# Attention of a four-layer kernel, step by step: one maximum, one step of scores and one of V in turn, with ScalarE writing all seeds

## The reference, cut to what matters

```python
N_HEADS = 16
HEAD_DIM = 64
q = (x @ Wq).reshape(b, s, N_HEADS, HEAD_DIM)
k = (x @ Wk).reshape(b, s, N_HEADS, HEAD_DIM)
v = (x @ Wv).reshape(b, s, N_HEADS, HEAD_DIM)
dot = jnp.einsum('bihd,bkhd->bhik', q, k)
w = jax.nn.softmax(dot / jnp.sqrt(jnp.float32(HEAD_DIM)), axis=-1)
a = jnp.einsum('bhij,bjhd->bihd', w, v)
return a @ Wo + bo
```

## Time and profile before

| what | us |
|---|---|
| median of three runs | 1858.48 |
| lowest and highest | 1855.24, 1868.66 |
| the profiled execution | 1866.86 |
| its span, first to last instruction | 1865.6 |
| PE busy in it | 1637.2 (88%) |
| POOL, DVE, ACT busy | 1306.1, 1302.3, 1154.1 |

### The profile page before, as it was taken

The page is one execution under the profiler, slowest core; times in us unless marked ns, Lnnn a source line. Parts: engine busy times, 40 slices in busy tenths (PEclk is TensorE's granted clock), DMA queues, the critical chain, the costliest instruction groups (busy, mean ns, idle before and its releaser), DMA issues.

```text
span 1865.6 us, 33807 instructions
## 1 busy us (share of the span) xinstructions
PE 1637.2 (88%) x12993; PEld 916.9 (49%) x12993; DVE 1302.3 (70%) x2075; ACT 1154.1 (62%) x1618; POOL 1306.1 (70%) x670
## 2 busy tenths in 40 slices
PE   3988863668999999999999999999999999995795
PEld 3767642654444444444444444444444444442475
DVE  2565667457777777777777777777777777763476
ACT  2455530355777777777777777777777777774323
POOL 2233331423998899998899998999998999995422
PEclk8587755778999999999999999999999999997698
DMA  8000000210000000000000000000000000000312
GB/s 244 3 3 4 3 1 8 61 44 1 1 1 1 1 1 1 1 1 1 1 1 1 1 1 1 1 1 1 1 1 1 1 1 1 1 1 25 101 40 74
DMA packets 33239, 29.72 MB, mean 16 GB/s; under 512 B 3676, under 2 KB 28752, under 8 KB 33080
## 3 DMA queue, kind: packets, MB, share of 16 engines
q1 hardware_dynamic: 24664, 19.38, 3.5%
q0 software_dynamic: 2496, 5.13, 0.8%
q10 hardware_dynamic: 5920, 3.04, 0.8%
HBM read 18.33 MB, written 9.21 MB: 15 GB/s over the span
## 4 chain that ended last, share of the span: by engine, by line
PE 61%; issue 12%; DVE 12%; ACT 7%; POOL 5%; DMA 1%; ACTq 1%; another core or an unknown queue 0%; POOLq 0%; DVEq 0%; SPq 0%
PE psum L1921 18%; PE psum L1906 13%; PE psum L1872 9%; DVE a_mx L2108 3%; ACT psum L2040 3%; POOL a_acc L2227 3%; PE psum L1887 2%; PE psum L1525 2%; PE psum L1929 2%; POOL y_rows L1090 1%; DVE a_Ql L2094 1%; PE psum L465 1%; ACT a_Qh L2002 1%; ACT a_Onh L2017 1%; PE psum L375 1%
## 5 line engine op out<-in xcount | busy, mean ns | idle before, releaser
L2227 POOL TENSOR_TENSOR a_acc<-a_acc,a_Pb 128x1024 f32<-128x1024 f32 x448 | 1065.8, 2379 | 108.4 <-ACT a_Pb L2025 52.7
L2108 DVE TENSOR_REDUCE a_mx<-psum 128x2 f32<-128x1024 f32 x512 | 622.0, 1217 | 194.6 <-PE psum L1872 191.4
L2025 ACT ACTIVATE a_Pb<-psum 128x1024 f32<-128x1024 f32 x512 | 496.8, 1023 | 296.3 <-PE psum L1906 291.1
L1921 PE MATMUL psum<-a_Pb,a_Vb 128*64 128x512 f32 x2048 | 494.1, 603 | 0.0
L2040 ACT ACTIVATE psum<-a_Mb 128x1024 f32<-128x1024 f32 x352 | 352.6, 1034 | 0.0
L1872 PE MATMUL psum<-a_Kh,a_Qh 64*128 64x512 f32 x1024 | 256.5, 491 | 26.1 <-DVE a_mx L2108 19.9
L1872 PEld LDWEIGHTS psum<-a_Kh,a_Qh 64*128 64x128 f32 x1024 | 103.1, 184 | 328.7 <-issue 305.6
L1921 PEld LDWEIGHTS psum<-a_Pb,a_Vb 128*64 128x64 f32 x2048 | 127.0, 136 | 222.5 <-issue 175.6
L1906 PE MATMUL psum<-a_Qh,a_Kh 64*128 64x512 f32 x1024 | 204.0, 394 | 1.8 <-ACT psum L2040 1.8
L1906 PE MATMUL psum<-a_Ql,a_Kh 64*128 64x512 f32 x1024 | 202.7, 390 | 0.0
L1906 PE MATMUL psum<-a_Qh,a_Kl 64*128 64x512 f32 x1024 | 202.7, 390 | 0.0
(11 more groups left out here) (389 smaller groups left out, 2013.8 us busy)
## 6 DMA issues: line engine op xcount, KB each, us to landing
x_rows<-att_raw ACTq DMA_DIRECT2D x2, 1483.5 KB, 25.4
g_w<-in_L_ffn_w_eDF_dram SPq DMA_DIRECT2D x2, 1408.0 KB, 8.7
r_W<-in_L_ffn_W_dram SPq DMA_DIRECT2D x1, 2048.0 KB, 14.1
r_tile_x<-x_rows SPq DMA_DIRECT2D x23, 64.5 KB
g_tile_x<-x_rows SPq DMA_DIRECT2D x23, 64.5 KB
y_all<-y_rows SPq DMA_DIRECT2D x4, 256.0 KB, 3.6
g_w<-in_L_ffn_w_eFD_dram SPq DMA_DIRECT2D x2, 512.0 KB, 9.4
g_xg<-y_rows SPq DMA_DIRECT2D x4, 256.0 KB, 3.9
```

Source lines behind the costliest of these rows:

```text
L1921: last = pe.matmul(ps[HEAD[h], B_O, :], b.Vb[:, p // 2 % 2, kc, at], b.Pb[:, step % BUFS, h * QT:(h + 1) * QT], start=(kc == 0), stop=(kc ...
L2025: act.activation(b.Pb[:, step % BUFS, :], ps[:, slot:slot + 2, :].rearrange("p a b -> p (a b)"), ACT.Exp, scale=SCALE).then_inc(S["probs"], 1)
L2108: v.tensor_reduce(b.mx[:, :, qc, quarter:quarter + 1], ps[:, bank:bank + 2, :], AX.X, ALU.max).then_inc(S[f"free{bank}"], 1)
L2227: g.tensor_tensor(b.acc[:, u, :], before, b.Pb[:, step % BUFS, :], ALU.add).then_inc(S["added"], 1)
```

## The change

The loop no longer goes by rounds of two steps but by single steps. In each step TensorE does the scores of the step, one maximum, the V products of the step two before, then the other job and the seed job where the step has one. The max jobs run further ahead: at step i of unit U it is job 7 + i of unit U+1 for i under 9 (AHEAD), and job i - 9 of unit U+2 from there on. In unit 0 the first seven steps have two maxima each, since nothing was made before the loop. ScalarE does an exp, then the seed of the step two ahead (which waits for that very exp), then copies; all seeds but the first of a unit are its own, and DVE has none. Jobs stand at steps 1 (k), 3 (q), 4 (sum), 11 (out), 14 (v and seed). The inversion stands at steps 4 to 7. The sizes, the matmuls and their number are the same.

```diff
--- before.py
+++ after.py
@@ -1672,51 +1672,49 @@
 NU = NT * P // QT
 PAIRS = 8
 UNITS = PAIRS * NU
-RN = NT // 2
-ROUNDS = UNITS * RN
-STEPS = 2 * ROUNDS
+STEPS = NT * UNITS
 BUFS = 8
 SCALE = 1.0 / float(np.sqrt(D))
 B_O, B_M, B_P = 4, 5, 7
 
 
-def misc_job(R):
-
-    U, d = R // RN, R % RN
+
+INVERT = (4, 5, 6, 7)
+
+AHEAD = 9
+
+
+def misc_job(step):
+
+    U, i = step // NT, step % NT
     p, qt = U // NU, U % NU
-    if d == 0 and p < PAIRS - 1:
+    if i == 1 and p < PAIRS - 1:
         return "k", p + 1, qt
-    if d == 1 and U:
+    if i == 3 and U < UNITS - 2:
+        return "q", U + 2
+    if i == 4 and U:
         return "sum", U - 1
-    if d == 4 and U < UNITS - 2:
-        return "q", U + 2
-    if d == 5 and U:
+    if i == 11 and U:
         return "out", U - 1
-    if d == 6 and p // 2 < PAIRS // 2 - 1:
-        return "v", p // 2 + 1, U % RN
+    if i == 14 and p // 2 < PAIRS // 2 - 1:
+        return "v", p // 2 + 1, U % 8
     return None
 
 
-def seed_job(R):
-    U, d = R // RN, R % RN
-    return ("seed", U + 1) if d == 7 and U < UNITS - 1 else None
-
-
-def max_jobs(R):
-
-    U, i = (R + 1) // RN + 1, (R + 1) % RN
-    return [("max", U, 2 * i + j) for j in range(2)] if U < UNITS else [None, None]
-
-
-
-SEED_DVE = (0, 5, 6, 7)
-
-
-def seeder(step):
-
-    if step % NT == 0 or step == 1:
-        return "pe"
-    return "dve" if step % 2 and (step // 2 - 1) % RN in SEED_DVE else "act"
+def seed_job(step):
+    U, i = step // NT, step % NT
+    return ("seed", U + 1) if i == 14 and U < UNITS - 1 else None
+
+
+def max_jobs(step):
+
+    U, i = step // NT, step % NT
+    first = NT - AHEAD
+    if U == 0 and i < AHEAD:
+        jobs = [(1, 2 * i), (1, 2 * i + 1)] if i < first else [(1, first + i)]
+    else:
+        jobs = [(U + 2, i - AHEAD) if i >= AHEAD else (U + 1, first + i)]
+    return [("max", *job) for job in jobs if job[0] < UNITS]
 
 
...
@@ -1888,39 +1882,35 @@
                                      start=(qc == 0), stop=(qc == 3), skip_group_check=True)
         end(last, 0)
 
-    def scores(R):
-        U, d = R // RN, R % RN
+    def scores(step):
+        U, kc, slot = step // NT, step % NT, 2 * (step % 2)
         p = U // NU
-        if d == 0:
-            freed(("seed", U))
+        if kc == 0:
             freed(("q", U))
             freed(("k", p, NU - 1))
-        for i in range(2):
-            kc, slot = 2 * d + i, 2 * i
-            at = slice(kc * P, (kc + 1) * P)
-            who, n = plan.seeded[2 * R + i]
-            if who != "pe":
-                pe.wait_ge(S[f"seeded_{who}"], n)
-            for n, (K, Q) in enumerate(((b.Kh, b.Qh), (b.Kh, b.Ql), (b.Kl, b.Qh))):
-                for h in range(2):
-                    last = pe.matmul(ps[:, slot + h, :], K[HEAD[h], p % 2, at], Q[HEAD[h], U % 3, :], start=False, stop=(n == 2), skip_group_check=True)
-            last.then_inc(S["scores"], 1)
-
-    def weigh(R):
-        U, d = R // RN, R % RN
+        if kc == 0:
+            freed(("seed", U))
+        elif step > 1:
+            pe.wait_ge(S["seeded"], seeds_of(step))
+        at = slice(kc * P, (kc + 1) * P)
+        for n, (K, Q) in enumerate(((b.Kh, b.Qh), (b.Kh, b.Ql), (b.Kl, b.Qh))):
+            for h in range(2):
+                last = pe.matmul(ps[:, slot + h, :], K[HEAD[h], p % 2, at], Q[HEAD[h], U % 3, :], start=False, stop=(n == 2), skip_group_check=True)
+        last.then_inc(S["scores"], 1)
+
+    def weigh(step):
+        U, kc = step // NT, step % NT
         p = U // NU
-        if d == 0:
-            freed(("v", p // 2, RN - 1))
+        if kc == 0:
+            freed(("v", p // 2, 7))
             if U:
                 pe.wait_ge(S["heads_out"], U)
-        for kc in (2 * d, 2 * d + 1):
-            step = NT * U + kc
-            pe.wait_ge(S["probs"], step + 1)
-            for h in range(2):
-                at = slice((p % 2) * P + h * D, (p % 2) * P + (h + 1) * D)
-                last = pe.matmul(ps[HEAD[h], B_O, :], b.Vb[:, p // 2 % 2, kc, at], b.Pb[:, step % BUFS, h * QT:(h + 1) * QT],
-                                 start=(kc == 0), stop=(kc == NT - 1))
-            last.then_inc(S["weighted"], 1)
+        pe.wait_ge(S["probs"], step + 1)
+        for h in range(2):
+            at = slice((p % 2) * P + h * D, (p % 2) * P + (h + 1) * D)
+            last = pe.matmul(ps[HEAD[h], B_O, :], b.Vb[:, p // 2 % 2, kc, at], b.Pb[:, step % BUFS, h * QT:(h + 1) * QT],
+                             start=(kc == 0), stop=(kc == NT - 1))
+        last.then_inc(S["weighted"], 1)
...
@@ -1960,25 +1950,21 @@
         if m % 2:
             values(0, m // 2)
     seed(0)
-    for _, U, m in max_jobs(-1):
-        maximum(U, m)
     for bank in range(NU + 1):
         pe.wait_ge(S[f"free{bank}"], plan.before[bank])
     pe.wait_ge(S["att_ready"], 1)
-    for R in range(ROUNDS):
-        late, early = max_jobs(R - 1)[1], max_jobs(R)[0]
-        if R and late:
-            maximum(*late[1:])
-        scores(R)
-        if early:
-            maximum(*early[1:])
-        if misc_job(R):
-            misc(misc_job(R))
-        if seed_job(R):
-            seed(*seed_job(R)[1:])
-        if R:
-            weigh(R - 1)
-    weigh(ROUNDS - 1)
+    for step in range(STEPS):
+        scores(step)
+        for _, U, m in max_jobs(step):
+            maximum(U, m)
+        if step > 1:
+            weigh(step - 2)
+        if misc_job(step):
+            misc(misc_job(step))
+        if seed_job(step):
+            seed(*seed_job(step)[1:])
+    weigh(STEPS - 2)
+    weigh(STEPS - 1)
     sums(UNITS - 1)
     output(UNITS - 1)
...
     def seed(step):
         U, slot = step // NT, 2 * (step % 2)
-        if plan.seeded[step][0] == "act":
-            bank, n = plan.at["seed", U]
-            act.wait_ge(S[f"free{bank}"], n)
-            act.wait_ge(S["probs"], step - 1)
-            act.activation(ps[:, slot:slot + 2, :].rearrange("p a b -> p (a b)"), b.Mb[:, U % 2, :], ACT.Copy).then_inc(S["seeded_act"], 1)
+        if step % NT == 0:
+            return
+        bank, n = plan.at["seed", U]
+        act.wait_ge(S[f"free{bank}"], n)
+        act.wait_ge(S["probs"], step - 1)
+        act.activation(ps[:, slot:slot + 2, :].rearrange("p a b -> p (a b)"), b.Mb[:, U % 2, :], ACT.Copy).then_inc(S["seeded"], 1)
...
@@ -2055,24 +2041,22 @@
     for qt in range(NU):
         keys(0, qt)
     queries(1)
-    for j in range(RN):
+    for j in range(8):
         values(0, j)
     guard(0)
-    for R in range(ROUNDS):
-        U, d = R // RN, R % RN
-        probs(2 * R)
-        probs(2 * R + 1)
-        if seed_job(R):
+    for step in range(STEPS):
+        U, i = step // NT, step % NT
+        probs(step)
+        if seed_job(step):
             guard(U + 1)
-        for step in (2 * R + 2, 2 * R + 3):
-            if step < STEPS:
-                seed(step)
-        key = misc_job(R)
+        elif step + 2 < STEPS:
+            seed(step + 2)
+        if i == 1 and U:
+            heads_out(U - 1)
+        key = misc_job(step)
         if key and key[0] in "qkv":
             {"q": queries, "k": keys, "v": values}[key[0]](*key[1:])
-        if d == 0 and U:
-            heads_out(U - 1)
-        if d == 3 and U:
+        if i == 8 and U:
             normalised(U - 1)
     heads_out(UNITS - 1)
...
@@ -2167,30 +2143,24 @@
         maximum(0, m)
     dve.wait()
     negate(0)
-    for _, U, m in max_jobs(-1):
-        maximum(U, m)
-    for R in range(ROUNDS):
-        U, d = R // RN, R % RN
-        late, early = max_jobs(R - 1)[1], max_jobs(R)[0]
-        if R and late:
-            maximum(*late[1:])
-        if d == 7 and U < UNITS - 1:
+    for step in range(STEPS):
+        U, i = step // NT, step % NT
+        if i == AHEAD and U < UNITS - 1:
             negate(U + 1)
-        if U and d in (2, 3):
-            invert(U - 1, 2 * d - 3)
-        if U and d == 4:
+        for _, unit, m in max_jobs(step):
+            maximum(unit, m)
+        if i == 2 and misc_job(step - 1):
+            keys(*misc_job(step - 1)[1:])
+        if i == 3 and misc_job(step):
+            queries(U + 2)
+        if U and i in INVERT:
+            invert(U - 1, INVERT.index(i))
+        if U and i == 8:
+            normalise(U - 1)
+        if U and i == 10:
             normalised_low(U - 1)
-        if early:
-            maximum(*early[1:])
-        if U and d in (1, 2):
-            invert(U - 1, 2 * d - 2)
-        if 2 * R + 3 < STEPS:
-            seed(2 * R + 3)
-        key = misc_job(R)
-        if key and key[0] in ("q", "k", "out"):
-            {"q": queries, "k": keys, "out": output}[key[0]](*key[1:])
-        if U and d == 3:
-            normalise(U - 1)
+        if U and i == 11:
```

34 lines of the change are left out of this document (10 added, 24 removed).

## The result

The changed kernel takes 1874.79 us (median of four runs, 1873.0 to 1883.45) against 1858.53 for the kernel before (four runs, 1855.24 to 1868.66): ratio 1.007, 95% interval 1.0042 to 1.0097. So it is a little slower, within the 1% that was the forecast's middle case; the forecast was 1868, the range 1856 to 1886.

The account below looks back on a forecast made before the run. TensorE was taken to bound the loop at 39.76 us a unit, POOL close behind at 37.9. Unit 0's +11.2 and later units' -1.6 gave +9.6 on 1858.5, so 1868 us, range 1856 to 1886.

Parts of the forecast that it names:

- middle case: Whole kernel: time within 1% (18.6 us) of the kernel before, chance 0.64.
- The steady step: TensorE's plain loop step: 0.33 + 1.01 + 0.33 + 0.23 + 0.23 = 2.13 us, 4.27 per two steps against 4.22.
- the value and seed jobs: TensorE's side jobs in each unit: value job worth 0.92 us, seed job 1.01.
- -1.6: Units after unit 0: 0.06 us gained per unit, over 27 units until POOL sets the pace.
- +11.2: Unit 0 of the loop: seven steps with two maxima each move its end to 490.9 from 479.70, +11.2 us.
- half clock until 449.5: Loop start: TensorE granted half clock until 449.5 us, so step 0 takes 4.0 us.
- a clock below 1.00 between 450 and 500: Sign of being wrong: TensorE's granted clock share falls below 1.00 between 450 and 500 us.
- half clock in unit 0: Rival, unit 0: waits bring 1.2 GHz, a double step takes about 5.9, five add 10 us: 1878; chance 0.08.
- ScalarE late: Rival, turn of a unit: V waits for heads_out, 0.5 us in each of 24 units, +12: 1880; chance 0.25.
- Free switches: Rival, each step: changed matmul shape costs nothing, step 0.25 shorter, POOL sets the pace, -36 us: 1822; chance 0.06.
- drain: Rival: the 0.43 after scores is drain, not wait; 4.7 us a unit, +127 on top: 1995; chance 0.04.

Follow-up runs that it names:

- half-reduced pair: Kernel before and changed kernel, each with DVE reducing only the first 256 of each 512 columns of the maxima: ratios to before 0.9703 and 1.0006.
- half-reduced kernel before: Kernel before with DVE reducing only the first 256 of each 512 columns of the maxima: 1809.69 us, ratio 0.9703, unit 38.03.
- first pair of profiles: Kernel before and changed kernel as first measured: medians 1858.53 and 1874.79 us, ratio 1.007.
- second run: Changed kernel run again without an edit: 1877.95 us, ratio 1.0077, unit 0 58.3, half clock 27.3 us.
- later batch: Both kernels run again without an edit: medians 1862.91 (before) and 1877.95 us (changed).
- repeated pair: Kernel before and changed kernel, each profiled again without an edit: spans 1859.7 and 1876.0 us, medians 1862.91 and 1877.95.

## Why the prediction was right, and where it was not

- **The steady step held.** Scores to maximum 0.23, maximum to V 0.33, V of one step 1.01, a step 2.13: all measured as worked out, two of them without a row of their own before. With a wait removed that was worth 1.73 a unit (half-reduced pair), the whole moved by 0.25: the new order's changes of shape give the rest back. Two small slips of the forecast stand beside this. By its starts a round of the earlier trace rows is 4.21 (1009.70 to 1013.91), not 4.22. And the changes of shape per two steps are four instead of two, so two are added and not three: maximum to V and V to scores, each twice. Their price is 0.35 per two steps, 4.26 against 3.91 in the half-reduced kernel before (1006.74 to 1008.78 up to V, and 1.87 for V), where the wait and the load that it exposed were worth 0.30.
- **The unit came out at 39.51, not 39.7.** The term mis-sized is the value and seed jobs, 0.92 + 1.01 = 1.93 in the sum and 1.74 measured. Behind a V, whose 1.01 already holds the switch, the first value matmul is followed after 0.22, the others after 0.12, and the seed job takes 0.93 (1007.65 to 1008.58) instead of 1.01. Over the rest of the loop it made -4.7 us out of the -1.6 that was forecast.
- **Unit 0 cost more than +11.2.** It was +14.6 in the first pair of profiles (55.9 against 41.3) and +17.6 in the second. The step that failed is "half clock until 449.5": the clock came back at 459.8 and, in the second run, at 467.4. One of the forecast's own signs of being wrong, a clock below 1.00 between 450 and 500, did show. The pattern itself was right. Step 0 lasted 4.05 (forecast 4.0), and a doubled step at full clock 4.05 (468.05 to 472.10, forecast 4.04):

```profile
468.05 0.50 PE L1898 MATMUL psum<-a_Qh,a_Kh 64*128 64x512 f32 x2
...
468.85 0.40 PE L1866 MATMUL psum<-a_Kh,a_Qh 64*128 64x512 f32 x2
470.66 0.50 PE L1866 MATMUL psum<-a_Kh,a_Qh 64*128 64x512 f32 x2 [1.41 <-DVE a_mx L2092]
471.09 1.08 PE L1911 MATMUL psum<-a_Pb,a_Vb 128*64 128x512 f32 x4
472.10 0.49 PE L1898 MATMUL psum<-a_Qh,a_Kh 64*128 64x512 f32 x2
```

  But step 2 at half clock lasted 6.12 (452.17 to 458.29), against the rival's 5.9. Steps 1 to 4 together took 22.0 (446.03 to 468.05), where the forecast's terms give 4.7 + 3 x 4.04 + 0.9 = 17.7: 4.3 more, and 1.0 of it came back as the loop's first scores were early (441.98 against 443.0). So the rival "half clock in unit 0", given 0.08, happened in part on top of the forecast; its "+10" was +4 here.

```profile
452.17 0.79 PE L1898 MATMUL psum<-a_Qh,a_Kh 64*128 64x512 f32 x2
...
455.66 0.79 PE L1866 MATMUL psum<-a_Kh,a_Qh 64*128 64x512 f32 x2 [1.42 <-DVE a_mx L2092]
456.38 1.97 PE L1911 MATMUL psum<-a_Pb,a_Vb 128*64 128x512 f32 x4
458.29 0.79 PE L1898 MATMUL psum<-a_Qh,a_Kh 64*128 64x512 f32 x2
```

- **The sum was right for the profiled pair by luck.** +14.35 and -4.7 give +9.65 at the loop's end, where +11.2 and -1.6 give +9.6: two errors of 3 us that cancel. The medians are further apart (+16.3, and +14.4 in the later batch). The span of the kernel before as first profiled, 1865.6, was 5.9 above its repetition: 2.2 ahead of the loop, 0.6 in it, 3.1 behind it. In the repeated pair, where the parts outside the loop differ by 3.4, unit 0 alone gives +17.6 and the rest -4.7. So a forecast made from the median needed a dearer unit 0, and 1868 stands 7 us below what was measured. The measured 1874.8 is in fact nearer to the rivals' 1878 (half clock) and 1880 (ScalarE late); units of 39.51 exclude the second.
- **ScalarE late** is a small term. heads_out comes just in time in every unit with a key job, as counted, and 0.5 late in units 28 to 30, which have none: 1.5 us in all, not 12. In unit 31 V waits 1.22, but there POOL sets the end.
- **Free switches and drain** fall. A step after V starts with the exposed load, 0.34 and not 0.23 (1004.70 to 1005.04), in the changed kernel as in the earlier trace rows. TensorE's weight loads have it starting with its matmul, after 0.81 without a load:

```profile
1004.70 0.19 PEld L1898 LDWEIGHTS psum<-a_Qh,a_Kh 64*128 64x128 f32 x2 [0.81 <-issue]
```

  The Trainium skill ("TensorE: Matmul & The Clock Gate", "Step-by-step: what each phase is for") has loads pulled ahead of running matmuls on one of two conditions: the row groups don't conflict, or the load goes to the background weight buffer. The forecast took this as hiding a load after V. But V's tile is 128*64, all 128 rows, so the first condition is not met, and whether the second one was, no row shows. The half-reduced kernel excludes drain: 0.22 once the reduction is short.
- Whether the waits at the loop's start are what keeps the half clock longer wasn't taken apart. Runs with longer or more waits there tend to have more of it (20.5 and 27.3 us with seven doubled steps; 10.2, 6.8 and 3.4 in the kernel before; 10.2 with seven doubled steps of half reductions, 6.8 and none at all with reductions of 64 columns). But it was 13.7 with seven full doubled steps and DVE's seeds, and 17.1 with only two, and one kernel differs by 6.8 between its own two runs. No run changed the clock alone, so this stays open.

## What to carry to other kernels

Where an engine's list is reordered to remove a wait, count the switches that the new order adds with the same care as the wait, and count them behind each kind of neighbour: here 1.7 us a unit or more were won and at least 1.5 lost. Look for places where a switch is paid anyway (a side job) and group the work there, but check what the job itself waits for: a job that overwrites a buffer belongs behind work that covers its reader. And price the first pass of a loop apart from the steady one, since work moved forward by a unit is paid there in full: one constant (how far ahead) was worth 15 us between the medians, 10.5 to 12.9 of them seen in unit 0, against the 4.7 that the new order won in all later units.

## What the runs showed of the hardware

- The stretch at 1.2 GHz after the loop's start is not a property of the kernel alone: the same kernel had 10.2 and 6.8 us of it in two runs, the changed one 20.5 and 27.3, while every steady unit repeated within 0.05 us.
- The same eight seed matmuls take 0.93 behind the value job (1007.65 to 1008.58), and 1.01 behind a product with V where no value job stands (1441.45 to 1442.46 in the changed kernel). A job's price depends on its neighbour.
- A ScalarE instruction that waits for the one right ahead of it starts 0.10 after its end (1001.42 + 1.02 = 1002.44, seed at 1002.54), while two that don't depend on each other overlap: seeds follow each other by 0.95 though each lasts 1.03.
